# Adaptive-norm transformer on one core: the second MLP's first half in the causal attention's buffers and banks, and earlier first loads

## What is computed

```
h = _layernorm(x) * (1 + ca) + sa
x = x + ga * L0_attn(h)      # 8 heads of 64: local attention (window 64) + routed "heavy" attention
h = _layernorm(x) * (1 + cb) + sb
x = x + gb * L0_ffn(h)       # 64 small MLPs of 16 (the first MLP)
h = _layernorm(x) * (1 + ca) + sa            # with the second layer's own modulation
x = x + ga * L1_attn(h)      # 16 heads of 16, q and k normalized and rotated, causal, softmax
h = _layernorm(x) * (1 + cb) + sb
x = x + gb * L1_ffn(h)       # 256 -> 1024 -> 256 with Gelu (the second MLP)
```

## Time and profile before

| | |
|---|---|
| median of 3 runs | 4031.28 us (4029.88 to 4032.38) |
| the profiled execution: its time, its span | 4027.47 us, 4025.5 us |
| busy PE, DVE, ACT, POOL | 3383.6, 2432.8, 1990.4, 1350.7 us (84, 60, 49, 34%) |
| mean granted clock of TensorE | 0.908 of full |
| DMA | 207.37 MB, mean 52 GB/s |
| batch to batch, third to fourth (first scores of the causal attention) | 1437.69 to 1905.38 us |

### The profile page before, as it was taken

One profiled execution on the slowest core, in us unless ns is written; L12 is line 12 of the kernel. 1 busy time (PEld: TensorE's weight loads), 2 busy tenths in 40 slices (PEclk: granted clock), 3 DMA queues, 4 the chain that ended last, 5 costly groups with the idle time before them and its releaser, 6 DMA issues. The chain is left out here.

```text
span 4025.5 us, 81682 instructions
## 1 busy us (share of the span) xinstructions
PE 3383.6 (84%) x30905; PEld 2026.9 (50%) x30905; DVE 2432.8 (60%) x5900; ACT 1990.4 (49%) x4715; POOL 1350.7 (34%) x1647
## 2 busy tenths in 40 slices
PE   6368789897799878998898978998799988999787
PEld 3235544465446544465545644465444654455444
DVE  6754767457663766547573675637674476736662
ACT  5213454645364553555455553655545553655544
POOL 4123442234422433224422443234422344224311
PEclk8579888999999988998889988999899988999888
DMA  7210230002400123102400024001220024000220
GB/s 238 85 37 14 56 105 29 16 13 65 112 16 26 32 58 88 28 13 56 110 25 14 22 56 112 17 24 50 78 62 16 13 64 112 16 26 17 65 69 7
DMA packets 233601, 207.37 MB, mean 52 GB/s; under 512 B 13776, under 2 KB 214224, under 8 KB 233176
## 3 DMA queue, kind: packets, MB, share of 16 engines
q1 hardware_dynamic: 229168, 192.61, 17.3%
q0 software_dynamic: 3328, 8.39, 0.7%
q10 hardware_dynamic: 720, 1.15, 0.1%
HBM read 123.83 MB, written 77.69 MB: 50 GB/s over the span
## 5 line engine op out<-in xcount | busy, mean ns | idle before, releaser
L2437 ACT ACTIVATE arena<-pb 128x512 f32<-128x512 f32 (+3 forms) x1536 | 664.1, 493 | 237.2 <-PE pb L1619 231.4
L2517 POOL TENSOR_TENSOR arena<-arena,small 128x512 f32<-128x512 f32 x256 | 288.1, 1128 | 497.1 <-DVE small L1796 495.5
L2240 ACT ACTIVATE arena<-arena,small 128x256 f32<-128x256 f32 x512 | 255.8, 500 | 375.1 <-DVE small L1779 374.7
L1619 PE MATMUL pb<-arena 98*32 98x512 bf16 (+3 forms) x4608 | 400.7, 343 | 39.0 <-ACT arena L2437 19.0
L2676 POOL TENSOR_SCALAR_AFFINE_SELECT arena<-arena 128x256 f32<-128x256 f32 x512 | 215.9, 425 | 561.9 <-ACT arena L2437 559.2
L1637 PE MATMUL pb<-arena,v 128*17 128x512 f32 (+3 forms) x3072 | 375.9, 495 | 21.1 <-POOL arena L2676 12.0
L1577 PE MATMUL pb<-arena 96*32 96x128 bf16 (+5 forms) x5280 | 359.8, 277 | 31.2 <-DVE arena L2093 10.3
L1779 DVE CUSTOM_DVE_ANT_0 arena<-pb,wmask 128x256 f32<-128x256 f32 x512 | 195.8, 419 | 218.3 <-PE pb L1313 211.2
L1577 PEld LDWEIGHTS pb<-arena 96*32 96x32 bf16 (+1 forms) x5280 | 187.1, 101 | 201.4 <-issue 63.7
L1313 PE MATMUL pb<-arena 128*128 128x256 f32 x1024 | 283.2, 402 | 5.0 <-issue 2.8
L1290 PE MATMUL pb<-hTf,wqkv 128*128 128x512 f32 (+1 forms) x640 | 246.3, 537 | 23.8 <-DVE hTf L1748 13.0
(11 more groups left out here) (346 smaller groups left out, 7263.1 us busy)
## 6 DMA issues: line engine op xcount, KB each, us to landing
arena<-split_q SPq DMA_DIRECT2D x64, 384.0 KB, 5.7
arena<-split_k SPq DMA_DIRECT2D x24, 768.0 KB, 6.7
split_q<-arena SPq DMA_DIRECT2D x64, 192.0 KB, 2.3
split_q<-arena SPq DMA_DIRECT2D x96, 128.0 KB, 2.0
split_k<-arena SPq DMA_DIRECT2D x64, 192.0 KB, 2.4
split_k<-arena SPq DMA_DIRECT2D x96, 128.0 KB, 2.1
arena<-split_k SPq DMA_DIRECT2D x24, 384.0 KB, 6.0
xn<-h_d SPq DMA_DIRECT2D x8, 1024.0 KB, 9.9
```

The source lines that it names most:

```text
L1619: mm = t.matmul(bank[bk][r:r + 32, 0:w_], ka[slot(c, g)][0:KA, h, kt_ * P + r:kt_ * P + r + 32], qa[slot(c, g)][0:KA, h, q0:NH], start=Tru ...
L2240: ins = s.activation(pm[n % 3][:, j], sm[n % 2][:, j], ACT.Exp, bias=nmx[:, 2 * sl + j:2 * sl + j + 1], scale=-1.0, accum_out=sml[:, 2 * s ...
L2437: s.activation(pp[pn % 4][:, h % 2, 0:w_], bank[n % 3][:, 0:w_], ACT.Exp).then_inc(a_exp1, 1)
L2517: g.tensor_tensor(pm[n % 3], pm[n % 3], rcl[:, 2 * sl:2 * sl + 2].unsqueeze(2).broadcast_to([P, 2, 2 * P]), ALU.mult).then_inc(p_norm0, 1)
```

## The change

1. **Buffers.** The first half of `mlp1` gets buffers of its own in the causal attention's zone: `g1` on the exponentials `pp`, the normalized rows and `hT2h` on `oc`, `hT2x`, `hT2l` and `xadd2` on `ocT`. It waits no longer for the chains' stores; ACT waits for both transposes before it overwrites the rows. `heavy` no longer waits for `t_w2` and `p_w2`, but for the stores of both odd and even chains. ACT waits for `mlp1` before the second half's exponentials. The maxima move to `small`, are cleared once, and DVE waits no longer for the local attention's last add.
2. **Banks.** `mlp1`'s first half takes banks 0, 1, 2. All fills, the first ones too, take banks 4 and 5 singly; `fill_pair` is gone, and the first row of maxima takes one of the two. Bank 3 is not zeroed any more.
3. **Loads.** Group 0 waits for the last local scores (`t_s0`), group 1 for the last weighted sum (`t_pv0`), and the ones stand behind group 1.
4. **Order.** `mlp1`'s first half is a fourth lane, `PACE` and `SIDE` have finer steps, and some gates move by a step or more.

```diff
-HROWS_BEHIND_MLP, ..., MLP_BEHIND_LIGHT = (6, 12, 11, 45, 13, 2)
-LOAD_STEP = 8
-LAG = 11
+HROWS_BEHIND_MLP, ..., MLP_BEHIND_LIGHT = (6, 12, 11, 49, 13, 1)
+LOAD_STEP = 7
+LAG = 9
...
-    lanes, gate = [[], [], []], {}
+    lanes, gate = [[], [], [], []], {}
-        lanes[1] += ... + [("chain", b, 0), ("chain", b, 2), ("mlp1", b, 0)]
+        lanes[1] += ... + [("chain", b, 0), ("chain", b, 2)]
+        lanes[3] += [("mlp1", b, 0)]
-        gate["mlp1", b, 0] = [(("att", b, 0), steps_of(("att", b, 0)) - 2), (("chain", b, 3), 42)]
+        gate["mlp1", b, 0] = [(("att", b, 0), steps_of(("att", b, 0)) - 2)]
+        if key[0] == "att" and key[2] == 1 and n == len(first_fills(1)) and not reached([(("mlp1", key[1], 0), 24)]):
+            return
...
-FIRST_BANKS, FIRST_ROW_BANK = ((0, 1), (4, 5)), 2
-        nm = [view([G1, TH, 4]) for _ in range(2)]
+        nm = [at(small, 256 + 64 * i, [G1, TH, 4]) for i in range(2)]
-        g1, xn2m = at(arena, ZONE_B, [FT, NH]), at(arena, ZONE_B + FT * NH, [TH, D])
-        hT2x = at(arena, HB + 1536, [KD, NH])
+        g1 = [at(arena, o, [FT, NH]) for o in (PP, ZONE_B)]
+        xn2m = [at(arena, o, [TH, D]) for o in (OC, ZONE_B + FT * NH)]
+        hT2x = [at(arena, o, [KD, NH]) for o in (OCT, HB + 1536)]
-        MLP1_BANKS = {0: (6, 7), 1: (7, 5, 6)}
+        MLP1_BANKS = {0: (0, 1, 2), 1: (7, 5, 6)}
...  (PE, fill)
-                        bk = max_bank() if no is None else FIRST_BANKS[no // 2 % 2][no % 2]
+                        bk = max_bank()
...  (DVE, heavy; ACT and POOL alike)
-                        v.wait_ge(t_w2, TH * (2 * b - 1))
-                        v.wait_ge(p_w2, TH * (2 * b - 1))
-                        v.wait_ge(split_out[1][1], 16 * SPLIT_DMAS * b)
+                        for j in range(2):
+                            v.wait_ge(split_out[1][j], 16 * SPLIT_DMAS * b)
...  (DVE, att)
-                        v.memset(bank[3], 0.0).then_inc(v_b3, 1)
-                        v.wait_ge(p_o0, 2 * TH * (b + 1))
-                        for j in range(2):
-                            ins = v.memset(nm[j], -3e38)
...
-                        if n % 2:
-                            fill_pair(*first_fills(c)[n - 1], n - 1)
+                        fill(*f)
...  (ACT, norm_half and att)
+                    s.wait_ge(t_n2, KD * H + KD)
+                    if c:
+                        s.wait_ge(t_w2, TH * (2 * b + 1))
+                        s.wait_ge(p_w2, TH * (2 * b + 1))
...  (SP, att)
-                        sp.wait_ge(t_o0, 2 * TH * (b + 1))
+                        sp.wait_ge(t_s0, 2 * UNITS * (b + 1))
+                        load_group(b, 0, 0)
+                        sp.wait_ge(t_pv0, 2 * UNITS * (b + 1))
+                    load_group(b, c, 1)
+                    if c == 0:
                         for ones in (...):
                             sp.dma_start(ones[KS:KA], ...).then_inc(ones_in, 16)
-                    for g in range(3):
-                        if c == 0 or g > 0:
-                            load_group(b, c, g)
+                    load_group(b, c, 2)
```

More of the change, by code:

```diff
@@ L170, in schedule @@
             credit -= 1.0
-        for lane in range(1, 3):
+        for lane in range(1, 4):
             if lanes[lane]:
                 key = lanes[lane][0]
-                due[lane] += SIDE[key[0], key[2]] if key[1] or key[0] != "chain" else 1.0
+                due[lane] += side_of(key, done.get(key, 0)) if key[1] or key[0] != "chain" else 1.0
             while due[lane] >= 1.0 and lanes[lane]:
@@ L2270, in heavy @@
                     if b:
[L2271 to L2272 removed]
+                        for j in range(2):
+                            s.wait_ge(split_out[1][j], 16 * SPLIT_DMAS * b)
                     for j in range(4):
@@ L2479, in mlp1 @@
                         gelu_tables[0] = True
-                        s.activation(g1[:, m], bank[banks[m % len(banks)]], ACT.Gelu, scale=alpha1[:, m:m + 1],
+                        s.activation(g1[c][:, m], bank[banks[m % len(banks)]], ACT.Gelu, scale=alpha1[:, m:m + 1],
                                      bias=cols[:, C_FB1 + m:C_FB1 + m + 1]).then_inc(a_g, 1)
```

112 lines of the change are left out of this document (46 added, 66 removed).

## The result

The changed kernel takes 3957.26 us, the median of four runs (3956.39 to 3962.4), against 4031.07 of the kernel before on the same chip. The ratio is 0.9822, with a 95% interval of 0.9807 to 0.9837: 72 us faster, between 66 and 78.

What follows compares the result with a forecast made beforehand. No single bottleneck: PE waits for the split_k load behind local attention and for DVE behind the second MLP's first half. Terms -24 - 4 - 17.5 + 9.6 - 2.6 = -38.5 us from 4031.28 gave 3993 us, range 3970 to 4022.

Steps and rivals of the forecast that it cites:

- Part 1: Local to causal attention: first loads issue earlier, first maxima start sooner, some given back to DVE; -24 us.
- Part 2: Second MLP's first half: with a third bank the third product no longer waits for a Gelu; -4 us.
- Part 3: Heavy attention's start: no wait for the MLP's buffers, DVE's clears and third row block earlier; -17.5 us.
- Part 4: Second half of causal attention: cost of single reductions and two banks for the fills; +9.6 us.
- Part 5: Order of steps: fewer Gelu table changes in the third batch, heavy attention one step earlier adds no work; -2.6 us.
- (a): Rival: chains or stores give half the gain of the first loads and heavy attention's start back; 4014 us, chance 0.18.
- (c): Rival: fills in two banks in turn make PE wait for DVE; 45 us slower, 4076 us, chance 0.07.
- (d): Rival: the last store or shared queue limits the loads, so first maxima start no earlier; 4032 us, chance 0.08.
- (b): Rival: PE's clock stays up behind the first maxima as PE stands less; 18 us more gain, 3975 us, chance 0.12.

Runs made afterwards that it cites:

- a_lane: Changed kernel with the second MLP's first half back in the lane ahead of heavy attention, without heavy attention's waits for it: ratio 0.9893 to the kernel before, +29 us against changed.
- b_single: Kernel before with all first fills one by one in banks 4 and 5, the first row of maxima in one of these: ratio 1.0010, +4 us.
- a_oldnums: Changed kernel with all old numbers of the order; lane, buffers, banks and loads as changed: ratio 0.9878 to the kernel before, +23 us against changed.
- b_loads: Kernel before with only the new waits of SyncE's first loads and the ones behind group 1: ratio 0.9924, -31 us.
- a_oldloads: Changed kernel with the old load waits and order of loads: ratio 0.9892 to the kernel before, +28 us against changed.
- b_warm: Kernel before with 14 unused PE products into bank 2 while PE would stand for the first split_k load: ratio 0.9983, -7 us.
- a_pace618: Changed kernel with pace 0.618, not 0.607, behind the last fills of the second half of causal attention: 4029 us, ratio 0.9996 to the kernel before.
- three old numbers: Changed kernel with old pace 0.632, norm start at step 45 and norm side pace 0.8: ratio 0.9921 to the kernel before, +40 us against changed.

## Why the prediction was wrong

The direction and the two places were right, the size was not. **Part 1** was forecast at -24 and is -28 to -31 by the two runs, its stretch -27.9. The store and the wait behind it came as worked out; PE starts 5.0 us after the keys' issue, where I took 6.0. The load itself is quicker: these eight loads landed after 5.7 to 6.2 us before and 4.6 to 6.6 now, median 6.0 and 4.9. The give-back to DVE is there, larger than the 1.0 us a batch of the sum: 19.7 us for 16.4 in the third batch. (The section on the anatomy of one DMA in the Trainium skill, "DMA: Bandwidth & Descriptors", from which the prediction's estimate of 3.8 us comes, is on DMAs issued by GpSimd. These loads are issued by SyncE, and the measured row, which the sum used, was the nearer one.)

**Part 2** was forecast at -4. The stage is 5.5 us shorter, but 4.7 of it is busy time, and with two banks it is no longer. The number came out by luck; the reason did not.

**Part 3** was forecast at -17.5. Undone, it costs 24 to 29 us, 20 of them in its stretch. The heavy product stands 3.4 us behind the MLP's last, as forecast. The working priced the new order of DVE, which is right, but the heading and the condition were the waits for buffers, and a_lane shows that without the waits and in the old place the time is the same: I named the 3.7 us after the permission, not the move. What lies beyond 20 is in other stages and is within the interval.

**Part 4** was forecast at +9.6. Alone it is +4, -3 to +10: inside its bounds, at the low end. One marker failed: DVE's busy time was to grow by 30 us and did not (2433.0 for 2432.8). The cost was sized rightly: added one by one, the reductions of the fills take 789.3 us, before 759.1, and without the change elsewhere (b_single) DVE's busy time grows by 17.0. But the busy time counts overlapping instructions once, and the clears of bank 3 and of the maxima, 5.4 us, went.

**Part 5** is the step that failed: "Heavy attention starts one step earlier, which moves work and adds none", -2.6 us. The order's numbers were put at nothing beyond that, and they are the larger part of what the forecast lacks: with the old numbers the changed kernel is 23 us slower, with the old pace alone 26. I compared the two orders for table loads and looked at nothing else that a shifted step meets. Parts 1 to 4 come to -36 in the forecast and a_oldnums, which has just these, to -49; parts 1 and 3, each larger than forecast by 4 to 12 us, can carry that rest.

The forecast also erred one level up. It took the kernel before as a neutral base and its 0.632 as a number that would serve both. The runs show that each kernel stands below the neighbours that were tried: the three other paces in the changed kernel and the two in the kernel before, each tried alone, made it slower by 21 to 70 us, while the whole new set did the kernel before no harm. With the old numbers the changed kernel comes to 4031 x 0.9878 = 3982, against 3995 for parts 1 to 4.

Of the rivals, (a) is wrong: part 1 reached the scores. (c) and (d) are out. **(b)**, the clock stays up, names what happened in more than half of the gain, 41 of 71 us, but not why. It had the clock fall because PE stood for the load, and priced that at 18 us. b_loads closes that gap, and the mean clock of its executions goes from 0.907 to 0.9105, a quarter of the way to 0.922; a_oldloads opens it again, and the clock goes back by as much, to 0.9185. b_warm fills it and gains 7 us. So this gap is a part of the clock's gain, and the smaller one. By the Trainium skill ("TensorE: Matmul & The Clock Gate", why this matters for kernels) idle gaps between bursts of matmuls drop the array to half rate. The trace of the kernel before agrees: the clock fell inside the 7.5 us behind the local attention (0.83 there, 0.77 behind it). That closing such a gap keeps the clock up, these runs do not bear out: with 1.9 us in its place the first maxima ran at 0.65. And shifting steps by one or two moved the mean of a kernel's executions from 0.922 to as low as 0.913 (a_pace618), with this gap closed in both.

One marker of the forecast was badly chosen: waits of the fills for DVE's reductions "that grow by more than 5 us a batch" were to show it wrong. They grew by 36.6 us, 4.6 a batch, just under the mark, and the kernel is 72 us faster. In b_loads alone 15.6 us of such waits came where the wait for the load had been.

**Open.** Why the clock falls in one order and not in the next is seen in these runs, not explained: the profile gives the clock of a stretch and not what set it, and executions of one program differ by up to 0.009. Nor is it settled why three old numbers cost more than all of them. In the first batch the first half of the attention is 8.2 us longer than before (75.9 for 67.7), 68.3 with all old numbers and 76.3 with the three; the lag of the chains is among what differs, and it was not tried alone. The losses of the undone parts, 28 + 29 + 26 = 83, come to more than the 72 gained, but each has an interval of about 11 us, so it is not shown that they overlap. That an old place or an old load also loses because the numbers no longer fit it was not tried: no undone part was timed with numbers of its own.

## What to carry to other kernels

Where one list of steps sets the order on all engines, a change and its order numbers are one thing: time the changed kernel at a few numbers around the old one before judging it, since shifts by one or two steps were worth up to 70 us here and the change itself, with the old numbers, some 50. Count busy time of PE apart from its idle time; where the instructions are the same and the busy time is not, look at the clock, and over all executions, not in the one trace. The wait removed from the code was worth here what moved in the order because of it, so try the two apart: as here, the old place without the wait.

## What was not expected of the hardware

The same 105 PE instructions in one stretch took 13.3 or 15.3 us of busy time, at granted clocks of 0.91 and 0.74, with less idle time in the slower one. The same program on the same chip had a mean clock of 0.903 in one execution and 0.909 in another, and took 4044 and 4028 us.

The first keys of each batch, 384 KB, landed 5.7 to 6.2 us after their issue (median 6.0) with the two loads of ones queued ahead of them, and 4.6 to 6.6 us (median 4.9) with the ones behind; with the old loads in the changed kernel it is 5.5 to 6.1 us again. For 768 KB the medians, 6.7 us before and 16.7 in the rows above, do not show a slower load. Before, 16 of these 24 loads took 6.4 to 7.2 us and the 8 of the second half's last group 13.9 to 17.2; the trace of the changed kernel holds only the landings of these 8, 13.7 to 17.3 us.
